# One attention part moved beside the last projection, and a section's opening loads issued in another order

## What is computed

```python
# layer 0 and 1: group norm, projection, 3x3 convolution, four scans, layer norm, gate, projection
def step(h, inp):
    u_t, dt_t, B_t, C_t = inp
    h = jnp.exp(dt_t[..., None] * A) * h + (dt_t * u_t)[..., None] * B_t[:, :, None, :]
    y = jnp.einsum('bkdn,bkn->bkd', h, C_t)
    return (h, y)
y = y1 + y2 + y3 + y4                      # four scan directions, brought back to image order
y = (y - mu) * jax.lax.rsqrt(var + 1e-05) * ln_w + ln_b
x = x + (y * jax.nn.silu(z)) @ out_proj_w.T
# layer 2 and 3, on tokens t of 96 channels, 6 heads of 16; no softmax
attn = jnp.einsum('bhnd,bhmd->bhnm', q, k) * D ** (-0.5)
y = jnp.einsum('bhnm,bhmd->bhnd', attn, v)
t = t + (y @ Wff + bff)
t = t + ffn(_ln_t(t))                      # 96 -> 384 -> 96, values rounded to fp8 and fp16
```

## Time and profile before

| | us |
|---|---|
| median of three runs | 11373.29 (11363.34 to 11389.22) |
| the profiled execution | 11397.64 |
| its span | 11395.9 |

### The profile page before, as it was taken

One profiled execution on the slowest core, in us unless ns is written; L12 is line 12 of the kernel. 1 busy time (PEld: TensorE's weight loads), 2 busy tenths in 40 slices (PEclk: granted clock), 3 DMA queues, 4 the chain that ended last, 5 costly groups with the idle time before them and its releaser, 6 DMA issues.

```text
span 11395.9 us, 94804 instructions
## 1 busy us (share of the span) xinstructions
PE 8819.1 (77%) x26272; PEld 2206.4 (19%) x26272; DVE 10173.2 (89%) x6087; ACT 6991.9 (61%) x10714; POOL 9736.9 (85%) x4231
## 2 busy tenths in 40 slices
PE   7876677876778777769777787888688876777767
PEld 2211111211112111212112121122111221122213
DVE  4899998999889999989999998899988999999973
ACT  5665555665556556677565765566755666667644
POOL 4899988899888999989988888888988889998860
PEclk9865577865779568769777787788677876777766
DMA  4666689566875566656776668956687566665550
GB/s 113 141 150 132 134 155 157 152 135 142 158 158 151 132 157 162 151 130 148 169 157 152 133 140 157 158 149 137 137 155 161 136 152 142 159 163 120 125 138 11
DMA packets 1779117, 1627.04 MB, mean 143 GB/s; under 512 B 1323598, under 2 KB 1324912, under 8 KB 1778588
## 3 DMA queue, kind: packets, MB, share of 16 engines
q1 hardware_dynamic: 1778588, 1620.97, 64.3%
HBM read 623.22 MB, written 192.15 MB: 72 GB/s over the span
## 4 chain that ended last, share of the span: by engine, by line
DVE 24%; issue 22%; PE 19%; POOL 18%; ACT 8%; DMA 4%; SPq 3%; DVEq 0%; POOLq 0%; ACTq 0%
POOL pr L1693 13%; DVE hs L1587 10%; DVE ps L1572 9%; DVE hs L1583 4%; PE ps L1084 3%; PE ps L1071 3%; PE ps L879 2%; PE ps L914 2%; PE ps L1062 2%; DMA dur<-us 2%; ACT dec L1336 2%; POOL dur L1707 2%; POOL bup L1707 2%; PE ps L1046 2%; POOL us L1684 1%
## 5 line engine op out<-in xcount | busy, mean ns | idle before, releaser
L1693 POOL TENSOR_TENSOR pr<-hs,crep 128x1024 f32<-128x1024 f32 x3072 | 7184.6, 2355 | 1175.9 <-DVE hs L1587 510.9
L1587 DVE TENSOR_TENSOR_SCAN hs<-dec,carry,ps 128x1024 f32<-128x1024 f32 x1728 | 4054.6, 2346 | 237.6 <-POOL pr L1693 13.4
L1071 PE MATMUL ps<-sbc,selb 96*128 96x512 bf16 x4608 | 1844.0, 492 | 1921.3 <-DVE hs L1587 1310.8
L1572 DVE TENSOR_TENSOR ps<-ps,dur 128x1024 f32<-128x1024 f32 x2304 | 2789.2, 1211 | 436.0 <-PE ps L1071 233.0
L1336 ACT ACTIVATE dec<-dtr,ac 128x1024 f32<-128x1024 f32 x2304 | 2611.0, 1137 | 486.5 <-DVE hs L1587 459.0
L1084 PE MATMUL ps<-pr,red 128*32 128x512 f32 x12288 | 2287.5, 827 | 19.7 <-POOL pr L1693 13.3
L1343 ACT ACTIVATE carry<-hs 128x1 f32<-128x1 f32 x2304 | 457.1, 199 | 2452.5 <-DVE hs L1587 2282.9
L1587 DVE TENSOR_TENSOR_SCAN hs<-dec,zero,ps 128x1024 f32<-128x1024 f32 x576 | 1351.5, 2346 | 72.2 <-ACT dec L1336 1.4
L879 PE MATMUL ps<-xb,tapw 96*96 96x512 f32 x2304 | 1176.8, 632 | 31.1 <-ACT sd L1168 28.5
L1071 PEld LDWEIGHTS ps<-sbc,selb 96*128 96x128 bf16 x4608 | 374.5, 108 | 4058.9 <-DVE hs L1587 2412.3
L1336 ACT ACTIVATE ps<-dtr,ac 128x1024 f32<-128x1024 f32 x768 | 848.6, 1105 | 421.8 <-DVE hs L1587 421.6
(11 more groups left out here) (228 smaller groups left out, 7622.2 us busy)
## 6 DMA issues: line engine op xcount, KB each, us to landing
dtr<-de SPq DMA_DIRECT2D x768, 512.0 KB, 8.1
dur<-us SPq DMA_DIRECT2D x768, 512.0 KB, 7.9
crep<-bc_d SPq DMA_DIRECT2D x512, 512.0 KB, 7.3
ust<-u_d SPq DMA_DIRECT2D x256, 384.0 KB, 6.1
y_d<-yst SPq DMA_DIRECT2D x768, 128.0 KB, 2.4
sd<-y_d SPq DMA_DIRECT2D x448, 192.0 KB, 4.6
brep<-bc_d SPq DMA_DIRECT2D x128, 512.0 KB, 7.2
u_d<-sd SPq DMA_DIRECT2D x64, 384.0 KB, 3.1
```

The lines of the kernel that those rows point to most:

```text
L1071: mm = pe.matmul(ps[:, SLOT + 2 * (n % RS) + hf, :], selb[:, i % GT // 2, :], sbc[:, w % 2, B * hf:B * (hf + 1)], start=True, stop=True)
L1572: dve.tensor_tensor(slot(n), slot(n), dur[:, 2 * (G % 2) + i % 2, :], ALU.mult).then_inc(bu_v, 1)
L1587: dve.tensor_tensor_scan(hs[:, n % RH, :], dec[:, others(n) % RD, :], slot(n), init, ALU.mult, ALU.add).then_inc(scan_v, 1)
L1693: pool.tensor_tensor(pr[:, n % RP, :], hs[:, n % RH, :], crep[:, q, :], ALU.mult).then_inc(prod_g, 1)
```

## The change

Three things are edited.

1. In the overlapped sections, post's opening on SP: instead of eight loads and x at once, one input (2 DMAs) at ticks 0, 2, 4 and 6 of the eight lead ticks, and x at tick 16 behind them (step 19 of the section's first window).
2. `load_du(0, w + 1)` is issued in step 18, directly behind `load_dt(0, w + 1)`, instead of step 20.
3. `attn` is split in two generators, `a1` (its first part) and `a2`. In the tail, `run_tail` runs post 7 and, from post's tick 39 on, a tick of `a1(6)` behind each tick of post; then the rest of `a1(6)`, `a2(6)` and attention 7. Attention 6's first part then takes a chunk every 13 ticks, one at a time, in a lane of its own (`tail_lane`: PSUM banks 0 and 5, buffers `bup` and `brep`). Its first chunk starts in the tick behind the projection add of post's first chunk. `alone` says that the lane is used by one chunk after the other, `banks` replaces `bank, bank + 1`.

All other attention parts keep their order and lanes.

```diff
+class TailLane:
+    def __init__(self, banks, squares, kv):
+        self.banks = banks
+        self.xa = squares[0:CH, 0:B]
+        self.sq = squares[0:CH, B:2 * B]
+        self.kvs = kv[:, 0:768].rearrange("p (t n) -> p t n", n=D)
...
+        tail_lane = TailLane((YB, PB), bup, brep)
...
+        def run_tail(stages):
+            (_, j), (_, first), (_, second) = plan[NSC + 1]
+            a1 = stages["a1"](first, False)
+            for tick, _ in enumerate(stages["post"](j, False)):
+                if tick >= POST_LANES * LANES:
+                    next(a1, None)
+            run(a1)
+            run(stages["a2"](first, False))
+            run(stages["attn"](second, False))
...
-        def a1_every(overlapped):
-            return A1_EVERY if overlapped else A1_LANES
+        def alone(N, overlapped):
+            return overlapped or N % 2 == 0
+
+        def a1_lane(c, N, overlapped):
+            return tail_lane if alone(N, overlapped) and not overlapped else lane(c, overlapped)
+
+        def a1_every(N, overlapped):
+            return A1_EVERY if overlapped else (A1_LANES if N % 2 else POST_LANES)
...
-                for n in range(4 if overlapped else len(ykt)):
-                    post_load(j, n, overlapped)
-                load_x(done, a["x"][b] if l == 0 else x_d[b])
-                for _ in range(post_lead(overlapped)):
+                if not overlapped:
+                    for n in range(len(ykt)):
+                        post_load(j, n, False)
+                    load_x(done, a["x"][b] if l == 0 else x_d[b])
+                for tick in range(post_lead(overlapped)):
+                    if tick % 2 == 0:
+                        post_load(j, tick // 2, True)
                     yield
...
+                        if overlapped and tick == 16 and c == 0:
+                            load_x(done, a["x"][b] if l == 0 else x_d[b])
...
                         if i == 18:
                             load_dt(0, w + 1)
-                        if i == 20:
                             load_du(0, w + 1)
...
-            run(beside(plan[NSC + 1], stages, False))
+            run_tail(stages)
...
-                side_banks(done)
+                if overlapped or l:
+                    side_banks(done)
+                else:
+                    pe.wait_ge(ye_a, NG * W)
+                    pe.wait_ge(z_a, 4 * W)
```

More of the change, by code:

```diff
@@ L680, in attn @@
                     yield
-                for tick in range(a1_ticks(overlapped)):
+                for tick in range(a1_ticks(N, overlapped)):
                     for c in range(C8):
-                        if overlapped and c < C8 - 2 and tick - a1_every(overlapped) * c == 6:
+                        if overlapped and c < C8 - 2 and tick - a1_every(N, overlapped) * c == 6:
                             sp.wait_ge(at_v, M + c + 1)
@@ L686, in attn, with a2 @@
                     yield
+            def a2(N, overlapped):
+                b, l = divmod(N, 2)
+                done = before["attn", N]
+                M = C8 * N
                 def t_load(p):
@@ L711, in attn @@
                     yield
-            stages = {"pre": pre, "post": post, "attn": attn}
+            def attn(N, overlapped):
+                yield from a1(N, overlapped)
+                yield from a2(N, overlapped)
+            stages = {"pre": pre, "post": post, "attn": attn, "a1": a1, "a2": a2}
             def load_u(w):
@@ L1667, in attn, with a2 @@
                     yield
-                for _ in range(a1_ticks(overlapped) + 4 + A2_TICKS):
+                for _ in range(a1_ticks(N, overlapped)):
+                    yield
+            def a2(N, overlapped):
+                M = C8 * N
+                for _ in range(4 + A2_TICKS):
                     yield
```

83 lines of the change are left out of this document (48 added, 35 removed).

## The result

| kernel | median, us | lowest to highest | runs |
|---|---|---|---|
| before | 11372.1 | 11352.8 to 11404.8 | 20 |
| after | 11391.4 | 11378.4 to 11412.0 | 20 |

The change made the kernel 19 us slower: the ratio is 1.0017, 95% interval 1.001 to 1.0023. Forecast was 11306, with a range that ends at 11368. The profiled execution of after took 11397.8 us, 6 above its median; that of before lay 25 above its own. So the two profiles show nearly the same span, and a difference between them is some 19 us too small. A second profile of before (in the experiments) helps with that.

What follows compares the result with a forecast made beforehand. The prediction took VectorE's scan loop, waiting for `dur` loads, as the bound, with a tail of 387 us behind. Terms 42 + 16 + 10 = 68 us off the profiled 11397.6, adjusted to the median, gave 11306 us, range 11260 to 11368.

Steps and rivals of the forecast that it cites:

- Part 1: Scan loop: `load_du` moved from step 20 to step 18 closes VectorE's `dur` gaps before windows, 42 us gained.
- 56.8 in reach: `dur` gaps at window starts outside the 2nd windows, where the room exceeds the gap: 56.8 us could go.
- only just covered: Side u and z loads behind the moved `load_du`: their slack of some 14 and 11 us just covers 6 us and landing.
- The lower bound of 15 us of gain: Part 1's low end: POOL or a blocked side load takes over the closed gaps, leaving 15 us.
- What is late next is POOL: Layer-0 openings: POOL, busy 311.16 us of 358, would be at about 95% with the gaps gone.
- the second rival: Loop: `dur` gaps turn into VectorE waiting for PE or POOL; gain only 20 us, 11353; chance 0.20.
- Part 2: Post's opening loads in overlapped sections: y pairs over four steps and x at step 19, 16 us gained.
- 2 us late is covered: Layer-0 openings: PE waits at step 12 for the second y pair, but steps 14 and 15 need no PE fill.
- The sign that came true for another reason: POOL's waits for `crep` were to grow by 10 to 30 us, with x ahead of `crep`.
- The slower rival: Seven openings: x ahead of `crep` stalls its whole landing time, 96 us; 26 us slower, 11399; chance 0.09.
- Part 3: Tail: attention 6's first part put beside post 7, 10 us gained.
- The sum at full clock: Tail with PE at 2.4 GHz: seven post periods take 90.4 us and the last chain 9, 23 us earlier.

Runs made afterwards that it cites:

- f1: `load_du` in step 18 against before, except in the 8th and 13th window of each section, where it stays in step 20: 11376.5 us, before 11383.5.
- e13_du18_2: Second profile of the kernel with only `load_du` moved to step 18, against before: profiled execution 11423.8 us.
- e12_before2: Second profile of the kernel before, nothing changed: profiled execution 11374.1 us.
- e2: Only `load_du` moved from step 20 to step 18, against before: median 11400.2 us, before 11380.0.
- e11: The whole change with `load_du` back at its old place in step 20, against before: median 11441.4 us, before 11380.5.
- e3: Only the opening edit (y pairs in four steps, x at step 19), against before: median 11424.3 us, before 11380.0.

## Why the prediction was wrong, point by point

- **Part 1, -42 forecast, +20 measured. This is the step that failed.** The room was read rightly: the gaps went (81.4 + 18.3 to 37.6 us in the loop), and they went where I had said (3.4 us are left of the 56.8 in reach). The room of 7.0 to 7.2 us before the 2nd window is counted from the end of `dtr`'s issue, not from POOL's product as I wrote (that would be 10.2 to 11.4); it is the right bound all the same. The cost of the move was not. I wrote that every instruction behind the moved wait counts, then named the u and z loads, found them "only just covered", and put it at a few us once or twice a section. The stores that `pre` issues in the same steps I did not name at all, nor attention's t load, though ACT's wait for the z store was already in the trace (8 waits, 18.0 us). By f1 the two windows of a section in which they fall are worth 27 us; five windows show them. And SP's wait for POOL, the only cost that I had in mind for what stands behind, was the smaller part: in window 23 it and the issue of `dur` are 2.7 us, the slower issue of the stores behind 1 MB of `dur` 5.5. Without these windows 7 us were gained of the 42, so the overlap failed elsewhere too: the next point. The lower bound of 15 us of gain held no loss: it should have reached below zero.
- **"What is late next is POOL".** It was PE, and then ACT. In e13_du18_2 VectorE waits 63 us more for PE and 41 more for ACT in the loop than in e12_before2, and no more for POOL. For ACT, the z store accounts for the four windows like window 23. PE's fills come in order behind its waits for side loads (20 us more for u); that this makes up all of the 63 is not shown. It is the mechanism of the second rival, *the gaps move*, which had 0.20 and 11353; its sum stopped at a gain since I gave it no price for the stores.
- **Part 2, -16 forecast.** The terms had the right places. The step-16 gaps for `dur` went, 18.3 us, but VectorE waits there for PE now, 2.69, 5.20, 5.03 and 4.65 us in the four openings, 17.6 in sum; I had "2 us late is covered". What I priced at 26.3 us (4.7 x 4 + 2.5 x 3), `crep` late behind x, shows as 20.2 us of VectorE's waits for POOL in the second windows, which are 21.8 us longer: that term held. The gain did not: the first windows, which the two parts together were to shorten by 43 us, got 18.4 shorter. The gaps before the 2nd windows gave 16.7 of it (24.7 to 8.0), those at step 16 gave 0.7. So the part came to +14 by the medians (+19 less +6), and the mis-sized term is its gain, at step 16 above all.
- **The sign that came true for another reason.** The `crep` row was to grow by 10 to 30 us through x and grew by 34. But e2 and e13_du18_2, with no edit of the opening, have 74.8 and 72.1 us there, and none of the 14 waits of after lies in a window behind x: the row's growth is due to `load_du` in step 18, and that it fitted the forecast is luck. The slower rival, x before `crep`, had its place right and its price too high: 96 us against 20.2.
- **Part 3, -10 forecast, 23.2 in the trace and 19 by the medians.** The sum at full clock, 90.4 + 9, met the measured 88.4 (11177.75 - 11089.32, seven periods) + 10.9 (the last chain), but in part by luck: the periods came out 2.0 us shorter and the chain 1.9 longer. What was wrong is the choice between the clocks. I took 0.85; the granted clock beside post was 0.96, with PE busy 76.75 us of 89, where before had 0.76 with 61.49 of 80. The 0.84 that I leaned on is a mean of two stretches of before, near 1.2 and at 2.4 GHz:

```profile
11145.00:11159.00 14.00, 12.02 (x22) 5.51 (x23) 5.19 (x4) 5.71 (x11) 0.00 (x0) 0.52 0.00 0
11160.00:11188.00 28.00, 24.79 (x132) 16.69 (x130) 5.89 (x14) 18.54 (x36) 0.00 (x0) 1.00 0.00 1
```

The Trainium skill (TensorE: Matmul & The Clock Gate, Part 1) says that the clock is gated by how busy the array has been recently. Both changes of the tail go that way, the rise within attention 6's first part and the 0.96 with it put beside post. The share of busy time in a row doesn't give the clock, though: the opening of layer 0 in after has 290.52 us of 358.10 busy at 0.71.

- **Part 2's queue.** The Trainium skill (DMA: Bandwidth & Descriptors, Queues, rings and completion order) says that each DMA engine consumes a queue's descriptors in ring order. It adds that a later one may finish before an earlier one, so "nothing of `crep` passes x" was more than it says. The traces agree as far as they go: POOL's first product of window 17 comes 7.6 us later in its window with x ahead of `crep`. They show besides that SP itself stands still: 11.97, 12.43 and 12.50 us for whatever it issues next.
- **The chances.** 0.09 for slower was for one mechanism alone. Two independent costs, each with a place in the trace, stood against a sum in which every gap was taken as time; the 89 us of `dur` gaps that went in the loop left nothing of their time.

What stays open: how much of the 57 us more that VectorE waits for PE on line 1571 in e13_du18_2 (12 more in the first pair of profiles) is the u load, the t load, or chance. Two executions of before differ by 21 us in that wait, so these profiles can't divide it. And e2 and f1 show the loss of the 8th and 13th windows together, not each by itself. Why e11 is 35 us above the sum of its parts is open as well.

## What to carry to other kernels

When an issue is moved forward on a shared queue, list every transfer that it now precedes, stores that free a buffer among them, and give each its waiter and slack before counting the gap that it closes. A gap at a window's start is worth only what the next wait in line leaves: here 60 us of `dur` waits bought nothing, and 28 us of them, taken by a swap with one store, bought 20. The load of x cost no less in step 19 or 23 than at the opening; for a large load in a busy queue, look for a stretch where nothing behind it is due, or leave it. And a wait that fits a forecast shows the forecast's reason only if a kernel without that edit lacks it.

## What the runs showed of the hardware

- A load of 1.5 MB held up the issuing queue itself: the next DMA on it took 11.97, 12.43 and 12.50 us to issue. The first two are a y store, which took 6.99 us at that place without x ahead (window 16 of before, against e3's 11.97) and 1.15 us in a quiet stretch. It isn't the size of one load alone: in after, two pairs of y loads of 192 KB each, from 1498.26, took 16.22 us to issue.
- Stores behind 1 MB of `dur` took 4.00 and 2.33 us to issue, 0.32 and 0.45 when they went first.
- TensorE's granted clock was 0.76 of 2.4 GHz beside post before and 0.96 with attention's first part put beside it (PE busy 61.49 of 80 us and 76.75 of 89). In the loop it was 0.71 with PE busy 290.52 of 358.10 us.
- Two executions of the same kernel 24 us apart had the same DMA waits to 4 us, one small one aside; most of the difference was in waits for PE.
